# Another order for the first turns of a fused cross-attention and mixture-of-experts kernel

## The reference

```python
xn  = layernorm(x)                                   # 32 x 128 x 128
q, k, v = xn @ Wq + bq, ctx @ Wk + bk, ctx @ Wv + bv  # 16 heads of 8
p   = softmax(where(mask == 0, -1e10, q @ k.T / sqrt(8)))
x   = x + tanh(g0) * ((p @ v) @ Wo + bo)
xf  = layernorm(x)
sh  = mean over 2 shared experts of gelu(xf @ sW1 + sb1) @ sW2 + sb2      # 128 -> 512 -> 128
moe = sum over the top 2 of 8 experts, weighted, of gelu(xf @ W1 + b1) @ W2 + b2
out = x + tanh(g1) * (sh + moe)
```

## Time and profile before

| | us |
|---|---|
| median of 3 runs (lowest, highest) | 495.75 (494.42, 496.45) |
| the profiled execution | 497.41 |
| its span, first to last instruction | 494.5 |
| busy in it: DVE, PE, ACT, POOL | 409.1, 398.6, 333.1, 319.5 |

### The profile page before, as it was taken

How to read it: one execution, slowest core, us unless ns; L and a number is a source line. 1 busy time by engine, 2 the same in 40 slices (tenths; PEclk the granted TensorE clock), 3 DMA queues, 4 the chain that set the end, 5 groups by cost and what they waited for, 6 DMA issues and landing times. The chain is left out here.

```text
span 494.5 us, 13519 instructions
## 1 busy us (share of the span) xinstructions
PE 398.6 (81%) x4611; PEld 300.7 (61%) x4611; DVE 409.1 (83%) x992; ACT 333.1 (67%) x658; POOL 319.5 (65%) x382
## 2 busy tenths in 40 slices
PE   0458789598689989886788887999899999999910
PEld 0235568477567777764553342444389999999910
DVE  7696798688877877789876889787579999999985
ACT  1122367477578868775676877788578888888834
POOL 9242222528499979868978776777027787777750
PEclk9999998899999989998889998999999999999975
DMA  8547658744234333353400111111303322345219
GB/s 224 134 100 185 169 169 205 190 110 98 56 84 109 80 92 81 94 177 130 174 29 21 49 53 45 49 50 48 91 13 93 98 94 88 97 131 175 77 33 306
DMA packets 71753, 53.19 MB, mean 108 GB/s; under 512 B 7473, under 2 KB 63548, under 8 KB 71688
## 3 DMA queue, kind: packets, MB, share of 16 engines
q1 hardware_dynamic: 64680, 42.99, 32.6%
q0 software_dynamic: 4544, 8.44, 4.9%
q10 hardware_dynamic: 2464, 0.91, 0.8%
HBM read 29.38 MB, written 24.33 MB: 109 GB/s over the span
## 5 line engine op out<-in xcount | busy, mean ns | idle before, releaser
L615 POOL DMA_INDIRECT yd<-Y,XR x78 | 86.5, 1109 | 45.3 <-issue 22.9
L698 ACT ACTIVATE PT<-pE,t_mbias,t_scl 128x512 f32<-128x512 f32 x128 | 97.1, 789 | 11.9 <-PE pE L834 11.7
L1214 DVE TENSOR_REDUCE t_MX<-pS 128x4 f32<-128x512 f32 x128 | 87.1, 684 | 20.4 <-PE pS L834 19.1
L590 POOL DMA_INDIRECT xs<-t_STG,t_pos x64 | 65.6, 1024 | 21.5 <-issue 14.2
L834 PE MATMUL pS<-t_K,t_Q 128*128 128x128 f16 x512 | 54.7, 236 | 10.3 <-DVE t_MX L1214 10.1
L1504 DVE SCALAR_TENSOR_TENSOR HR<-G,t_sc,HR 128x512 f16<-128x512 f32 x78 | 58.6, 751 | 2.8
L1096 PE MATMUL pAtt<-t_W2h,HR 128*128 x624 | 59.1, 219 | 1.2 <-DVE HR L1504 1.2
L1473 DVE SCALAR_TENSOR_TENSOR HH<-H,t_sc,HH 128x512 f16<-128x512 f32 x64 | 48.0, 759 | 9.7 <-ACT HH L744 7.6
L1096 PE MATMUL pAtt<-t_W2l,HR 128*128 x312 | 54.4, 219 | 0.0
L834 PE MATMUL pE<-t_Q,t_K 128*128 128x128 f16 x512 | 52.5, 228 | 0.9 <-ACT PT L698 0.5
L775 ACT ACTIVATE G<-pS,t_b1T,t_inv 128x256 f32<-128x256 f32 x78 | 39.9, 562 | 17.3 <-PE pS L1084 17.3
(11 more groups left out here) (269 smaller groups left out, 1019.9 us busy)
## 6 DMA issues: line engine op xcount, KB each, us to landing
xs<-t_padrow SPq DMA_DIRECT2D x10, 516.0 KB, 5.5
XR<-xs SPq DMA_DIRECT2D x39, 129.0 KB, 2.4
scr<-QKS SPq DMA_DIRECT2D x16, 256.0 KB, 2.3
t_Q<-scr SPq DMA_DIRECT2D x16, 256.0 KB
t_K<-scr SPq DMA_DIRECT2D x32, 128.0 KB
t_STG<-in_W SPq DMA_DIRECT2D x7, 512.0 KB, 5.5
YY<-yd SPq DMA_DIRECT2D x14, 256.0 KB, 5.1
t_X<-in_x SPq DMA_DIRECT2D x4, 512.0 KB, 5.2
```

What stands on the lines that cost most here:

```text
L590: g.indirect_dma_start(k.xs, bass.IndirectOffsetOnAxis(ap=pos[:, n:n + 1], axis=0), k.PAY[:, n, :], None).then_inc(h.di[q], 16)
L615: g.indirect_dma_start(k.yd, bass.IndirectOffsetOnAxis(ap=XR[u][:, q, D:ROW], axis=0), Y[u][:, q, :], None, bounds_check=2 * T - 1, oob_is ...
L698: act.activation(PT[:, m % NPT], pE[g % 2][:], ACT.Exp, bias=k.mbias[:, bt:bt + 1], scale=k.scl[:, bt:bt + 1]).then_inc(s.exp, 1)
L1214: v.tensor_reduce(out=MX[:, n % G // 4, m % 2, m // 2::2], in_=pS[n % 2][:], axis=AX_X, op=ALU.max).then_inc(s.max, 1)
```

## The change

What it does, by part:

- **Prologue.** DVE no longer takes the maxima of ctx chunks 0 and 1 there; all four are taken after the barrier.
- **Zeroes.** Buffers 2 and 3 of Q and V are cleared by ACT (four activations of scale 0, then two of ones) between its first copy (XCT) and `queries_keys(0)`, instead of by DVE in turn 0.
- **PE start.** The first projection of queries and keys comes behind the two small products that broadcast the maxima.
- **DVE order.** The deviations of x's chunks 1 to 3 are computed in turn 0, followed by weight pieces 0 and 1; pieces 2 and 3 in turn 2 where the deviations stood; the other six, the tops and the second scales earlier by up to one turn.
- **SP order.** x chunks 2 and 3 and weight pieces 0 and 1 are issued ahead of the first store of `scr`; then two pieces a turn from turn 1. The tops are stored in turns 3 and 6, not 4 and 7. Each pair of pieces has its own semaphore.
- **Shifts.** In turn 2 alone (t < LAG), PE transposes the shifts and ACT copies them ahead of the transposes and projection of pair 3, which now wait for that copy.

Cut to its core:

```diff
@@ prologue, vector
                 first_deviations(v, link, k, 0, CHUNK, tmpv, tmpn)
-                for n in range(2):
-                    v.wait_ge(k.s_c[n], 16)
-                    absmax(v, k.mx[:, 5 + n:6 + n], k.CC[n].rearrange("p a b -> p (a b)"))
@@ layer, sync
-    TOPS_STORED = (LAG + 1, LAG + 4)
+    TOPS_STORED = (LAG, LAG + 3)
-            load_tokens(2)
+            for n in range(2, NT // CHUNK):
+                load_tokens(n)
+            for n in range(2):
+                load_weights(n)
-                if t == 0:
-                    load_tokens(3)
-                for n in {1: range(0, 1), 2: range(1, 3), 3: range(3, 5), 4: range(5, 8), 5: range(8, 10)}.get(t, ()):
+                for n in {1: range(2, 4), 2: range(4, 6), 3: range(6, 8), 4: range(8, 10)}.get(t, ()):
                     load_weights(n)
@@ scalar
             transposed(0)
+            for u in range(2, NB):
+                eights = view(k.ones, 0, [0, 8], [1, P])
+                act.activation(k.V[u][:].rearrange("p a b c -> p (a b c)").rearrange("p (n d) -> p n d", d=P), eights, ACT.Copy, scale=0.0)
+                act.activation(k.Q[u][:].rearrange("p a b -> p (a b)").rearrange("p (n d) -> p n d", d=P), view(k.ones, 0, [0, 16], [1, P]),
+                               ACT.Copy, scale=0.0).then_inc(s.zz, 1)
+            act.wait_ge(s.zz, NB - 2)
+            for u in range(2, NB):
+                ins = act.activation(view(k.V[u], HD, [64, 16], [48, 2], [1, HD]), view(k.ones, 0, [0, 16], [HD, 2], [1, HD]), ACT.Copy)
+            ins.then_inc(s.z, 1)
             queries_keys(0)
                     if g == 2 and t < LAG:
+                        if b:
+                            shifts_out(t)
                         transposed(t + 1)
                         queries_keys(t + 1)
@@ tensor
-                if i > LAG:
-                    pe.wait_ge(s.t2, i - 2)
+                wait(pe, s.t2, i - 2)
-            project_queries_keys(0)
             pe.wait_ge(s.md, 1)
             pe.matmul(pA[1][:, 0, 0:5], k.ones[0:5, :], k.mxd[:], start=True, stop=True)
             pe.matmul(pA[1][:, 1, 0:B], k.ones[:], k.maskT[:], start=True, stop=True).then_inc(s.ma, 1)
+            project_queries_keys(0)
                     if g == 1 and t < LAG:
+                        if b:
+                            transpose_shifts(t, a)
                         transposes(t + 1, 0)
@@ vector
-            for n in range(2, NT // CHUNK):
+            for n in range(NT // CHUNK):
                 v.wait_ge(k.s_c[n], 16)
-                    if t == 0 and g < 2:
+                    if t == 0 and g < NT // CHUNK - 1:
                         chunk_statistics(g + 1)
-                        chunk_moments(g + 1)
-                    if t == 0 and g == 2:
-                        other_buffers()
+                        last = chunk_moments(g + 1)
+                        if g == NT // CHUNK - 2:
+                            link(last)
+                            other_deviations()
+                    if t == 0 and g in (4, 5):
+                        weight_piece(g - 4)
+                    if t == LAG and g == 6:
                         first_tops()
+                    if (t, g) in ((LAG + 1, 5), (LAG + 2, 2), (LAG + 2, 7), (LAG + 3, 2)):
+                        weight_piece(PIECES + ((LAG + 1, 5), (LAG + 2, 2), (LAG + 2, 7), (LAG + 3, 2)).index((t, g)))
+                    if t == LAG + 3 and g == 5:
                         second_tops()
+                    if t == LAG + 4 and g == 7:
                         second_scales()
                         if t == 2:
-                            other_deviations()
+                            weight_piece(2)
+                            weight_piece(3)
```

More of the change, by code:

```diff
@@ L313, in layer @@
     names = ("xn T XT qk qk32 hi lo ST S max mp nmT t2 exp pv ev tk at bt cp op x "
-             "st vp vev dv bias bvr any gb scl wm wk wb ws wh wl mb mr md ma qs st1 rs z")
+             "st vp vev dv bias bvr any gb scl wm wk wb ws wh wl mb mr md ma qs st1 rs z zz")
     s = Parts(**{n: sem("a_" + n) for n in names.split()})
@@ L412, in load_weights @@
                     src, dst = w.rearrange("e d h -> d e h"), k.weight_pieces[n].rearrange("p (e h) -> p e h", h=HID)
-                sp.dma_start(dst, src).then_inc(k.s_w[2 * which + (n % PIECES >= 3)], 16)
+                sp.dma_start(dst, src).then_inc(k.s_w[n // 2], 16)
             def store_tops(n):
@@ L710, in body @@
                     if g == 2 and t < LAG:
+                        if b:
+                            shifts_out(t)
                         transposed(t + 1)
                         queries_keys(t + 1)
-                    if g == 3 and b:
+                    if g == 3 and b and t >= LAG:
                         shifts_out(t)
@@ L882, in transpose_shifts @@
                 pe.wait_ge(s.mp, t - 1)
-                if t < LAG:
-                    pe.wait_ge(s.qk32, t + 2)
-                elif a:
+                if a:
                     pe.wait_ge(s.vev, t + 1)
@@ L1155, in chunk_moments @@
                 return ins
[L1157 to L1162, removed]
             def other_deviations():
-                chunk_statistics(3)
-                link(chunk_moments(3))
                 first_deviations(v, link, k, CHUNK, NT, tmpv, tmpn)
@@ L1171, in weight_piece @@
             def weight_piece(n):
[L1173 to L1174 removed]
+                v.wait_ge(k.s_w[n // 2], 16 * 2)
                 return absmax(v, mxw[:, n:n + 1], k.weight_pieces[n])
@@ L1404, in body @@
                 for g in range(G):
-                    if t == 0 and g < 2:
+                    if t == 0 and g < NT // CHUNK - 1:
                         chunk_statistics(g + 1)
-                        chunk_moments(g + 1)
-                    if t == 0 and g == 2:
-                        other_buffers()
-                    if t == LAG and g > 4 or t == LAG + 3 and g in (1, 3, 5):
-                        weight_piece(g - 5 if t == LAG else PIECES + g // 2)
-                    if (t, g) in ((LAG + 1, 3), (LAG + 4, 2)):
-                        weight_piece(3 if t == LAG + 1 else PIECES + 3)
-                    if t == LAG + 1 and g == 5:
+                        last = chunk_moments(g + 1)
[5 more added lines that the diff above has]
+                    if t == LAG and g == 6:
                         first_tops()
@@ L1417, in body @@
                         first_scales()
-                    if t == LAG + 4 and g == 4:
+                    if (t, g) in ((LAG + 1, 5), (LAG + 2, 2), (LAG + 2, 7), (LAG + 3, 2)):
+                        weight_piece(PIECES + ((LAG + 1, 5), (LAG + 2, 2), (LAG + 2, 7), (LAG + 3, 2)).index((t, g)))
+                    if t == LAG + 3 and g == 5:
                         second_tops()
-                    if t == LAG + 5 and g == 5:
+                    if t == LAG + 4 and g == 7:
                         second_scales()
@@ L1561, in program @@
         k.kmd = dram("kmd", (T,), F16)
-        k.s_w = [outer.enter_context(nc.semaphore(f"w_loaded{n}")) for n in range(4)]
+        k.s_w = [outer.enter_context(nc.semaphore(f"w_loaded{n}")) for n in range(PIECES)]
         k.s_empty = outer.enter_context(nc.semaphore("slots_empty"))
```

2 lines of the change are left out of this document (removed).

## The result

The changed kernel takes 488.0 us (median of 4 runs, 487.26 to 488.65) against 496.1 for the kernel before (4 runs): a ratio of 0.984, 95% interval 0.981 to 0.987. That is 8 us faster. The forecast was 10 us, to 485.7, with a range of 482.0 to 490.5. The profiled execution has a span of 485.5 us against 494.5: 9.0 us less.

The account below looks back on a forecast made before the run. DVE, the fullest engine, was taken to bound the attention stage. Gains at the start, turn 2 and turns 3 to 8, less 0.6 for SP's hold, sum to 10.0 us: 495.75 becomes 485.7, range 482.0 to 490.5.

Parts of the forecast that it names:

- it reaches the end: Behind turn 8 nothing changes, so the whole gain stays; the rival that it doesn't: 492, chance 0.05.
- the light turns at 11.3: Rival: PE and POOL keep light turns from going under about 11.3 us; gain 7.6, so 488.1; chance 0.17.
- SP's hold: SP waits for kwm's landing, delaying shifts and loads in turns 4 and 7: 0.6 us; rival in full 489.4, chance 0.08.
- their use comes more than 3 us after: Shifts and loads that SP delays in turns 4 and 7 are needed over 3 us later, so cost 0.6 of 0 to 4.3.
- Start: Prologue to ACT's scaling: barrier work starts 1.55 us sooner, scaling gains 0.2 us.
- 0 to 0.5: Cost of DVE's fuller run up to the first maximum, at 40.1 us, in turns 0 and 1; taken 0.
- Zeroes on ACT: Before ACT's scaling: two buffers 5.9 us and ones 0.8, done at 25.9, hidden by 0.15 us.
- Turn 2: Shifts of pair 0 ahead of pair 3's transposes; DVE's maximum at 52.45 instead of 53.54, a gain of 1.1 us.
- Bulk loads: 2.1 MB issued at 17 to 19.5 us is through at about 28, before the scratch's first store; taken as nothing.
- the rival of the slow bulk: Bulk at 80 GB/s or less delays the scratch's first store; 12 us lost, 497 and more; chance 0.03.
- Turns 3 to 8: With less DVE work and waiting, turns 3 to 8 become 10.6, 10.6, 13.0, 10.6, unchanged and 10.9 us.
- My 4.5 us for turn 5: DVE's 4.48 us wait for maxima through DRAM goes; turn 5 falls from 17.5 to 13.0 us.

Follow-up runs that it names:

- run 9: Changed kernel with both stores of the maxima three columns wide and issued ahead of their turn's bulk loads: 486.2 us, ratio 0.980.
- run 12: The changed kernel itself, measured again on the chip of run 9: 488.8 us, ratio 0.985.
- run 2: Changed kernel with the loads of the maxima behind the loads of Q and K, and second scales in turn 8, step 5: 485.6 us, ratio 0.976.
- run 5: run 2 with weight pieces 0 and 1 in turn 2 and the first projection ahead of the two small products: 486.2 us, ratio 0.982.
- run 10: run 9 with weight pieces 0 and 1 in turn 2 and the first projection ahead of the two small products: 486.6 us, ratio 0.981.
- run 11: run 10 with the shifts of pair 0 behind pair 3's transposes and projection again: 485.8 us, ratio 0.980.
- run 3: Changed kernel with the maxima stored a turn later again (turns 4 and 7) and second scales in turn 8: 492.5 us, ratio 0.989.
- run 7: run 2 with the second store of the maxima, and its load, three columns wide (12 bytes a partition, not 4): 489.0 us, single run.

## Why the prediction was right, and where its size was off

The direction and the mechanism held: the gain comes from the fill and the turns behind it, it is in the turns that I named but for turns 4 and 7, and it reaches the end. The sum was 2 us too large against the medians, 1 us against the spans of the two profiles. The measured 488.0 is the number of a rival, the light turns at 11.3 (488.1), but by luck: its turns were not seen (below). That the whole came within 2 us is in part luck too, since a hold that cost more met light turns and a turn 2 that were shorter than forecast.

- **SP's hold: the term that was mis-sized.** I took 0.6 us of 0 to 4.3. By the traces it stretched turns 4 and 7 by 1.1 and 2.7 us, of which turn 8 gave 1.0 back. Taking its length away gains 2.6 us (1.3 to 3.9, runs 9 and 12); with the loads off the way of the shifts and the scales later, the ratio falls from 0.984 to 0.976 (run 2), some 4 us, though these intervals just overlap. The step that failed is "their use comes more than 3 us after": in turns 4 and 7 PE had nothing else to do 1.1 and 2.8 us before the shifts were there, and in turn 7 DVE's scales wait on the same chain. The landing was longer too: 7.6 and 10.2 us, where I had 6.8 and at most 8.6. What I made of a rule of the Trainium skill (DMA: Bandwidth & Descriptors, Queues, rings and completion order), that the increment lands only after the earlier writes of the same DMA engine, was too little: I let it give a cost of 0. In the kernels of the change the first store lands 7.0 to 8.1 us after issue behind 1 MB of weights and 4.0 to 4.6 ahead of them, as the rule would have it; but 1.4 to 3.0 us of the longer time is SP's issue of the store itself (0.34 to 0.45 in front), and no run separates the rest from a store whose own transfer starts late. What hid the effect in the earlier trace rows is the width of the second store.
- **Start.** Forecast 0.2 us sooner and the first shifts at the same moment; they came 1.0 later in the first profile, and 1.5 to 2.4 later in the others with the same turn 0 (barrier at 17.35 to 18.6). Most of it is the barrier, which came at 17.32, not 16.5. SP's last issue before it ended 0.34 us later than in the kernel before, and the barrier fell 0.74 us behind that end, where it had fallen 0.26 behind DVE's; in run 12 it was alike, in the other runs SP ended later still (17.2 in run 2). The scaling and the small products are then as late as the barrier, to 0.3 us. The rest is DVE, whose turn 0 was too full: the deviations took 4.2 us (35.26 to 39.48) where I took 2.8, so the first maximum stood behind the weight pieces, 1.4 later than before. The maxima made up for a part, as the scores were there already: from the barrier to the first shifts it is 30.7 us in the first profile and 31.1 in run 12, where the forecast has 30.5. That is a cost of 0.2 to 0.6 us, where I had 0 to 0.5.
- **Zeroes on ACT.** Right: 1.05 and 1.90 us for 1,024 and 2,048 columns, forecast 1.04 and 1.92; done at 26.26, and the scaling waits for PE. They are hidden, by 0.35 us. The Trainium skill (ScalarE: Activation LUTs, Rules for kernel authors) has about 0.3 us plus 0.83 ns an element for an activation whose bias is a pointer operand, which would make 1.15 and 2.00; these have no such operand, so they don't test that rule.
- **Turn 2.** Forecast 1.1 for the order; 2.6 in the first profile, 1.1 in the second (run 12). What differs between these two is PE's speed. The scores of one step, of the first profile and of run 12:

```profile
55.69 0.40 PE L842 MATMUL pS<-t_K,t_Q 128*128 128x128 f16 x4 [0.28 <-DVE t_MX L1212]
```
```profile
56.14 0.61 PE L842 MATMUL pS<-t_K,t_Q 128*128 128x128 f16 x4 [0.19 <-DVE t_MX L1212]
```

The four products last 0.40 us where the granted clock is 1.00, 2.4 GHz, and 0.6 where it is 0.50, 1.2 GHz (the first profile has both on record, 0.50 from 44.9 to 55.2 us). The windows of run 12 print 1.00 for its turn 2 too, but there is nothing behind that: its trace holds no record of the clock before 60.0 us, and a stretch without one is printed as 1.00. The kernel before has none before 60.6 us, so the 1.00 of the first window of the earlier trace rows is no measurement either; its products took 0.61 to 0.63 us until then. So I go by the products. They turn fast, and stay so past the turn, at 55.7 us in the first profile, at 60.9 in run 12, and at 60.9 in the kernel before. With shifts first, turn 2 takes 11.2 to 11.4 us in the five traces where that is before 57.1, 11.7 in run 5 (57.9), and 12.4 to 12.9 in the four where it is after 60. So some 1.5 of the 2.6 is that. The other 1.1 is what I had forecast: from the first shifts to the first maximum of pair 1 it is 5.5 us in the changed kernel and 6.5 before, as DVE, with 2.3 us of weight pieces instead of 6.4 us of statistics and deviations, now waits for PE there (2.48 us). It is the work taken off DVE, not the shifts' place, as far as runs 5, 10 and 11 can tell. That maximum started at 53.54, as before, not at 52.45, since the first shifts were late.
- **Bulk loads.** Right: the first store of the scratch went at 29.56 and Q was loaded 2.6 us after it, as before; the rival of the slow bulk is out. By windows, 20 to 22 us of the changed kernel (to the earlier trace rows), DMA moves 222 GB/s:

```profile
20.00:22.00 2.00, 0.00 (x0) 0.00 (x0) 1.97 (x3) 2.00 (x3) 0.37 (x1) 1.00 0.83 222
```

- **Turns 3 to 8.** Turn 3 10.06 for 10.6, turn 5 11.99 for 13.0, turn 6 10.55 for 10.6, turn 8 10.34 for 10.9: better than forecast by 2.2 us together in the first profile. The rival of the light turns at 11.3 is out by turn 3, 10.1 in both profiles; turn 6 took 12.3 in the second, with a mean clock of 0.86, and 11.4 in runs 2 and 9. My 4.5 us for turn 5 measured 5.5; runs 2 and 3 (12.15 and 17.33) give 5.2.

Why the narrow store lands late, and what makes PE's clock rise at 54 us in some executions and at 61 in others, stays open.

## What to carry to other kernels

Where a queue engine waits for a round trip, everything behind it in its order waits too: cost the hold by what the first waiting consumer needs, at the longest landing seen and not the median, and look whether the same hold was harmless before only because something else stalled then. A small store whose landing is waited for goes ahead of the bulk loads and, where it is as narrow as 4 bytes a partition, is made wider, even with columns that nobody needs: here 12 bytes were enough. Work moved into a gap ahead of the critical chain must fit it at the durations that it has beside the other engines' work (the deviations: 4.2 us, not 2.8). And ask whether a clock that a profile prints was on record in that stretch at all.

## What the hardware showed

- A store of 128 rows of 4 bytes to DRAM landed 7.7 to 10.2 us after its issue (ten traces), one of 128 rows of 12 bytes, as the same second store, in 3.8 to 4.7 (four). In the very same place of the program it was 10.2 and 4.7 (runs 2 and 7).
- The same 12-byte rows behind 1 MB of weights took 7.0 to 8.1 us to land, of which SP's issue of the store itself was 1.4 to 3.0 us; ahead of the weights they took 4.0 to 4.6, the issue 0.34 to 0.45.
- Right behind two weight pieces, SP's issue of a 256 KB store lasted 1.7 to 2.0 us, and 2.7 to 4.2 us with the load of the maxima ahead of the pieces besides (4.15 in run 2, at 77.92); it takes 0.4 where nothing is ahead.
- Four TensorE products of 128 x 128 take 0.40 us at a granted clock of 1.00 and about 0.61 at 0.50. The clock rose between 54 and 61 us, in traces of nearly the same program, and with shifts first turn 2 took 11.2 to 11.4 us where it rose before 57, 12.4 to 12.9 where it rose at 60 or later.
